# Two attention layers: constant rows and the first batch's rows in pieces, GpSimd's key rotation behind the statistics, bulk loads behind maxima transfers

## What is computed

```
x = x + xattn0(layernorm(x), ctx, ctx)      # rotary embedding on q and k, linear position bias per head
x = x + ffn0(layernorm(x))                  # every token goes to its best expert
x = x + xattn1(layernorm(x), ctx, ctx)      # learned q, k, v and output projections
x = x + ffn1(layernorm(x))                  # every expert takes its 128 best tokens of a batch
```

## Time and profile before

| | |
|---|---|
| median of 3 runs | 1086.34 us (1085.2 to 1089.04) |
| profiled execution | 1078.34 us, span 1076.5 us |
| layer 0's attention, in the span | 0.7 to 277 us |
| layer 1's attention, in the span | 515 to about 800 us |
| TensorE busy | 944.4 us, 88% |
| VectorE, ScalarE, GpSimd busy | 56%, 48%, 28% |
| mean granted TensorE clock | 0.953 |

### The profile page before, as it was taken

One profiled execution on the slowest core, in us unless ns is written; L12 is line 12 of the kernel. 1 busy time (PEld: TensorE's weight loads), 2 busy tenths in 40 slices (PEclk: granted clock), 3 DMA queues, 4 the chain that ended last, 5 costly groups with the idle time before them and its releaser, 6 DMA issues. The chain is left out here.

```text
span 1076.5 us, 17358 instructions
## 1 busy us (share of the span) xinstructions
PE 944.4 (88%) x6842; PEld 650.2 (60%) x6842; DVE 605.6 (56%) x1011; ACT 513.6 (48%) x777; POOL 300.5 (28%) x280
## 2 busy tenths in 40 slices
PE   0159999899798999999779999999979999999993
PEld 0023334343576999999653444444449999999993
DVE  7678979794432111110586766979314836655553
ACT  1027777678423322332326775767633035445550
POOL 5467843000001222221132122000000245554222
PEclk9999999899869999999997999999987999999997
DMA  9978372500439999996884061320006224555316
GB/s 159 234 206 200 94 195 58 96 4 4 153 134 373 325 338 345 339 345 220 186 202 91 33 119 62 73 51 4 4 2 236 79 59 133 141 169 146 98 21 175
DMA packets 52148, 158.96 MB, mean 148 GB/s; under 512 B 7792, under 2 KB 27888, under 8 KB 41392
## 3 DMA queue, kind: packets, MB, share of 16 engines
q1 hardware_dynamic: 35952, 121.96, 38.7%
q0 software_dynamic: 12912, 29.63, 11.3%
q10 hardware_dynamic: 3216, 6.43, 1.6%
HBM read 116.18 MB, written 40.76 MB: 146 GB/s over the span
## 5 line engine op out<-in xcount | busy, mean ns | idle before, releaser
L786 DVE TENSOR_REDUCE a_row_max<-ps_ring 128x2 f32<-128x1024 f32 x256 | 308.9, 1222 | 79.0 <-PE ps_ring L581 76.6
L719 ACT ACTIVATE a_probs<-ps_ring 128x1024 f32<-128x1024 f32 x256 | 260.7, 1022 | 102.1 <-PE ps_ring L596 100.2
L615 PE MATMUL ps_out<-a_probs,a_vaug 128*32 128x256 f32 x2048 | 166.7, 399 | 2.5 <-ACT a_out_sb L725 1.5
L581 PE MATMUL ps_ring<-a_ka,a_qa 52*128 52x512 f32 (+1 forms) x512 | 120.1, 473 | 54.4 <-DMA a_ka<-scratch_k_scr 44.2
L596 PE MATMUL ps_ring<-a_qa,a_ka 56*128 56x512 f32 (+1 forms) x512 | 131.7, 511 | 5.7 <-DMA a_qa<-a_max_t 3.7
L1056 ACT ACTIVATE e_hid<-ps_ring,e_wts 128x128 f32<-128x128 f32 x184 | 52.3, 368 | 120.2 <-PE ps_ring L1156 86.2
L596 PEld LDWEIGHTS ps_ring<-a_qa,a_ka 56*128 56x128 f32 (+1 forms) x512 | 49.1, 188 | 98.6 <-issue 67.3
L581 PEld LDWEIGHTS ps_ring<-a_ka,a_qa 52*128 52x128 f32 (+1 forms) x512 | 51.5, 199 | 86.9 <-issue 38.9
L1445 ACT ACTIVATE e_hr<-ps_ring 128x512 fp32r<-128x512 f32 x64 | 38.3, 598 | 118.9 <-PE ps_ring L1516 118.9
L1516 PE MATMUL ps_ring<-e_xt,e_wr 128*128 128x512 f32 x384 | 88.7, 390 | 0.4 <-DVE e_xt L1584 0.4
L615 PEld LDWEIGHTS ps_out<-a_probs,a_vaug 128*32 128x32 f32 x2048 | 41.1, 109 | 78.4 <-issue 72.2
(11 more groups left out here) (229 smaller groups left out, 1275.0 us busy)
## 6 DMA issues: line engine op xcount, KB each, us to landing
e_wts<-in_w SPq DMA_DIRECT2D x23, 1156.0 KB, 8.2
e_wts<-in_w SPq DMA_DIRECT2D x23, 1024.0 KB, 7.7
e_wf<-in_w SPq DMA_DIRECT2D x16, 1024.0 KB, 5.3
scratch_q_scr<-a_qst POOLq DMA_DIRECT2D x36, 256.0 KB, 3.2
a_qa<-scratch_q_scr SPq DMA_DIRECT2D x24, 384.0 KB, 10.2
a_ka<-scratch_k_scr SPq DMA_DIRECT2D x24, 384.0 KB, 12.2
scratch_k_scr<-a_kst POOLq DMA_DIRECT2D x9, 512.0 KB, 15.8
scratch_xl<-e_xn SPq DMA_DIRECT2D x8, 512.0 KB, 5.0
```

Of the source, the lines that this page charges most:

```text
L581: ins = pe.matmul(to[:, par], qa[rows, b % 2, g, p, qt * P:(qt + 1) * P], ka[rows, b % 2, g, p], start=True, stop=True)
L615: ins = pe.matmul(m.ps_out[VW * h:VW * (h + 1), cols], vaug[:, b % NV, kc, HG * g + h], probs[:, t % 3, h, cols], start=(kc == 0 and half ...
L719: nc.scalar.activation(probs[:, t % 3, 2 * half:2 * half + 2], unit("s", n), ACT.Exp, scale=HD ** -0.5).then_inc(exp_done, 1)
L786: dve.tensor_reduce(row_max[:, s % 3, qt, :, p], unit("m", n), AX.X, ALU.max).then_inc(mx_read, 1)
```

## The change

1. The constant rows come in three pieces: piece 0 is slot 0 of the batches, group 0; piece 1 is slot 0, groups 1 to 3; piece 2 is slot 1. In layer 0 each piece is six DMAs (16, 48 and 64 KB each), in layer 1 two. Piece 0 is issued without the wait for x; piece 1 by GpSimd behind query tile 0 (layer 0) or at once (layer 1); piece 2 in step -4, ahead of query tile 3. TensorE waits for each piece at its first use instead of for all.
2. Batch 0's rows are loaded in three parts: group 0, group 1, groups 2 and 3, twelve DMAs instead of eight.
3. In layer 0 GpSimd waits for `stats_done` 2 (the statistics of batches 1 to 3) before `keys(1)`.
4. A batch's loads are issued in steps 16b - 15 and 16b - 11 and behind the maxima transfers of their step (before: 16b - 14 and 16b - 12, ahead of them; for batch 1 steps 2 and 4). For batch 1 and for every second part they also wait for a maximum product, `mx_full`. Layer 1 loads batch 1's keys there too.
5. `normed` does its two tiles one step apart. Layer 0 gets 30 idle multiplications ahead of the loop.

```diff
         def groups(b, part):
-            cut = 1 if b == 0 else 2
-            return (0, cut) if part == 0 else (cut, NG)
+            if b == 0:
+                return ((0, 1), (1, 2), (2, NG))[part]
+            return ((0, 2), (2, NG))[part]
...
-                        if b >= 2:
+                        if b == 1:
+                            sp.wait_ge(mx_full, 8 + 1)
+                        elif b >= 2:
                             sp.wait_ge(st_full, 8 * NG * (b - 1))
-                    if layer == 1 and b >= 2:
+                    elif b:
+                        sp.wait_ge(mx_full, 8 * (NG * (b - 1) + groups(b, part)[0]) + 1)
+                    if layer == 1 and b:
                         load_keys(b, part)
...
-                for part in range(2):
+                for part in range(3):
                     load(0, part)
-                if layer == 1:
-                    for part in range(2):
-                        load_keys(1, part)
                 for t in steps:
...
-                        for part in range(2):
-                            if t == (2 if b == 1 else 16 * b - 14) + 2 * part:
-                                load(b, part)
                     for job in ended.get((t, 1), []):
                         if job[0] == "m":
                             load_max(job[1])
+                    for b in range(1, B):
+                        for part in range(2):
+                            if t == 16 * b - 15 + 4 * part:
+                                load(b, part)
...
-                if layer == 0:
-                    pool.wait_ge(x_in[0], 16)
...
+                def constant_rows(piece):
+
+                    f, g0, g1 = ((0, 0, 1), (0, 1, NG), (1, 0, NG))[piece]
+                    kinds = ((ka, QK_ROWS, "k_bias"), (qa, QK_ROWS, "q_bias"))[:2 if layer == 0 else 0] + ((ka, M_ROWS, "k_select"),)
+                    for dst, at, name in kinds:
+                        for par in range(2):
+                            src = dram[name] if name == "k_select" else dram[name][par]
+                            pool.dma_start(dst[par * HALF_P + at:par * HALF_P + at + 4, f, g0:g1].rearrange("r g p t -> r (g p t)"),
+                                           src[:, g0:g1].rearrange("r g p t -> r (g p t)")).then_inc(rows_in[piece % 2], 16)
+
+                constant_rows(0)
...
                     queries(0)
+                    constant_rows(1)
                     values(0)
+                    pool.wait_ge(stats_done, 2)
+                else:
+                    constant_rows(1)
                 for t in steps:
+                    if t == -4:
+                        constant_rows(2)
...
-                pe.wait_ge(rows_in, 16 * n_rows)
+                if layer == 0:
+                    keep_awake(30)
...
-                        if t == max(q_at[i] - 3, steps[0]):
-                            normed(i)
+                        for j in range(2):
+                            if t == max(q_at[i] - 4 + j, steps[0]):
+                                normed(i, j)
```

More of the change, by code:

```diff
@@ L207, in attention @@
             bo_ready = sem("bo_ready")
-        rows_in = sem("rows_in")
+        rows_in = [sem(f"rows_in{i}") for i in range(2)]
         vaug_set = sem("vaug_set")
@@ L235, in attention @@
         n_ctx = 2
-        n_rows = 6 if layer == 0 else 2
+        row_pieces = (0, 1, NG)
+        n_kinds = 3 if layer == 0 else 1
         k_scr = dram["k_scr"]
@@ L328, in rows_in_place, with landed @@
                                         scr[b].rearrange("r (d h) t -> (r d) (h t)", d=HD)[:, cols])
+                def landed(b, part):
+                    if b:
+                        return loaded[part]
+                    return (first_loaded, *loaded)[part]
                 def load_keys(b, part):
                     for par in range(2):
-                        rows_in_place(ka, k_scr, b, part, par).then_inc(k_loaded[b % 2][part], 16)
+                        rows_in_place(ka, k_scr, b, part, par).then_inc(landed(b, part), 16)
                 def load(b, part):
@@ L526, in keep_awake @@
                     for _ in range(n):
-                        pe.matmul(misc[:, 0:P], m.ident[:], m.ident[:], start=True, stop=True)
+                        pe.matmul((misc if layer else m.ps_out)[:, 0:P], m.ident[:], m.ident[:], start=True, stop=True)
                 def job_at(job, n):
@@ L570, in maxima_scores @@
                     b, g = s // NG, s % NG
-                    for part in range(2):
+                    for part in range(2 if b else 3):
                         if w == 0 and g == groups(b, part)[0]:
-                            if layer == 0:
-                                pe.wait_ge(loaded[part], 64 * (b + 1))
-                            else:
-                                pe.wait_ge(loaded[part], 32 * (b + 1))
-                                pe.wait_ge(k_loaded[b % 2][part], 32 * (b // 2 + 1))
+                            if s == 0:
+                                pe.wait_ge(first_loaded, 64)
+                            else:
+                                pe.wait_ge(loaded[part if b else part - 1], 64 * (b + 1))
+                            if s in row_pieces:
+                                piece = row_pieces.index(s)
+                                pe.wait_ge(rows_in[piece % 2], 32 * n_kinds * (piece // 2 + 1))
                     to = take_unit("m", n)
@@ L702, in _ @@
                     if job == (norm_kind, 0):
-                        normed(0)
-                        normed(1)
+                        for i in range(2):
+                            for j in range(2):
+                                normed(i, j)
                     act_job(job)
```

24 lines of the change are left out of this document (12 added, 12 removed).

## The result

| | before | after |
|---|---|---|
| median of the runs shown | 1087.69 us (1085.2 to 1089.82) | 1060.26 us (1053.83 to 1061.54) |
| profiled execution | 1078.34 | 1059.8 |
| its span | 1076.5 | 1058.0 |

The ratio is 0.9737 (95% interval 0.9691 to 0.9783). The kernel is faster, but the median lies 9.4 us under the forecast of 1069.7 and 3.7 us under the range. The profiled executions differ by 18.5 us, close to the 16.6 of my sum; the medians differ by 27.4.

A forecast was written before the change was run, and what follows sets the result against it. TensorE, mostly 90% busy, was taken to lose time waiting in the ramp, where constant rows hold the DMA queue, and for later transfers. Terms -8.2 - 5.6 + 1.9 + 1.0 - 3.2 - 2.0 - 0.5 = -16.6: median 1069.7 us, range 1064 to 1079.

The forecast's parts named there:

- Bulk behind the maxima: Step 8 scores wait for a maxima transfer behind bulk loads of batch 1; moving the loads gains 3.2 us (0 to 3.2).
- Constant rows in pieces: Start of layer 0: smaller pieces free SyncE's queue, so query stores land 8.2 us earlier (6.9 to 10.9).
- Three parts: Ramp: group 1's rows land right behind group 0's, the 8.4 us wait goes; 5.6 us gained, 3 if late.
- What is late next: Ramp: slot 0's maxima transfer, queued behind bulk loads, becomes the limit; 1.9 us given back (0 to 5).
- Piece 2, and the wait for statistics: GpSimd's chain and 384 KB of constant rows in layer 0: the wait costs nothing; 1.0 us lost for both (0 to 8).
- Rival (a): New wait in step 4 or 8 from late batch 1 rows or maxima; 6 to 8 us lost, about 1077; chance 0.20.
- (d): Slower: the last 384 KB of constant rows block the queue longer than their size suggests; 1088 to 1090; chance 0.07.
- `normed` in halves: ScalarE's 1.41 us piece split over two steps shortens TensorE's waits for an exponential; 2.0 us gained (0.5 to 3.5).
- Idle multiplications: TensorE at about 13 us: 0 on the path, ramp products stay at half speed; 2.2 us if they woke it.
- Layer 1: Layer 1's start: less queued ahead of the y rows, but VectorE sets the path; 0.5 us gained (-1 to 1.5).
- Rival (b): Start: input loads themselves, not the constant rows, cause the slow stretch; stores still land at 42, 1077 to 1079; chance 0.08.
- Rival (c): More is won: stores land at 31.3, no maxima wait, clock rises early; 1064 or less; chance 0.13.

The follow-up runs named there:

- the second profile: The kernel before, unchanged, measured and profiled once more: 1087.4 us, ratio 1.0032; its profiled execution took 1081.81 us.
- the context experiment: Kernel after with batch 2's context loaded behind slot 0's maxima transfer instead of ahead of it: 1062.47 us, beside 1062.31.
- the constant rows whole: Kernel after with all six constant-row transfers at the start and one TensorE wait for them, as before: 1068.73 us, ratio 0.9847.

## Why the prediction was wrong

**The step that failed is *Bulk behind the maxima*,** 3.2 us (0 to 3.2). It went wrong twice. I put the wait of 3.2 us into step 8 of batch 0; but the earlier trace rows has 0.43 there, and the wait of 3.2 stands in the timeline of before at batch 3:

```profile
205.12 0.80 PE L596 MATMUL ps_ring<-a_qa,a_ka 56*128 56x512 f32 x2 [3.23 <-DMA a_qa<-a_max_t]
...
207.28 0.79 PE L596 MATMUL ps_ring<-a_qa,a_ka 56*128 56x512 f32 x2
...
210.32 0.50 PE L596 MATMUL ps_ring<-a_qa,a_ka 56*128 56x512 f32 x2
```

And I took the wait for its price. Behind it the pairs stay at 0.80 us for 5 us, and the slot is 17.0 instead of 11.65: 5.3 us in this execution. Others lose more (18.6 and 15.3 in the second profile). Measured alone the part is 9.8 us, and 6.6 more than I gave it brings the sum from -16.6 to -23.2, against -23.0 measured. The split agrees: beside each other this part alone took 9.8 us off and the rest 13.0 (predicted 13.4). In the kernel after it is 16.4, because there the scores come 11.5 us earlier and batch 1's loads, in their old place, only 5.8 (74.96 instead of 80.78, behind GpSimd's chain), so that step 8 runs into them. It was a mechanism that I had named, with its place and its price wrong; the same wait of 3.2 also went into my time for step 8 (27.7 less 3.2 behind the scores), which came 27.1 us behind them, as before (27.7).

**The choice of the base failed with it.** I worked on a profile 8 us under the median and applied its sum to the median as if the 8 us were a constant. They were not: part of them were the losses that this change removes. In the second profile of before these are the 3.3 us more in the two slots; how much they are in the other executions no profile shows. The profile moved by 18.5 and the median of all executions by 23.0.

*Constant rows in pieces* (-8.2, range 6.9 to 10.9, less 2.6). Right in mechanism, too large: 5.75 us in the first loads of the two profiles (6.4 between the means of three profiles with the pieces and three without), 5.1 in the scores when only this part is undone, because both pieces held others up more than I took. Piece 0 kept the inputs back by 1.6 to 2.2 us (I took 0, at worst 2.6), and piece 1 the stores by about 5 (2.7: 34.0 against 31.3). And the part is worth nothing without the others. Why so few bytes hold others back, by the 4 partitions of each transfer, by GpSimd's queue or by something else, no run tested.

*Three parts* (-5.6). From first product to scores it was 25.3 and is 19.7 us: 5.6. The wait of 8.4 is gone.

*What is late next* (+1.9). Scores at 62.4 predicted, 62.84 measured, but this was luck: the maxima transfer was good for less than 1 us (the context experiment). What made the sum come out is that the pieces won less.

*Piece 2, and the wait for statistics* (+1.0, "the wait costs the path nothing"). The statistics were done at 32.75 instead of 31. The wait doesn't only cost nothing; it is worth 4 us of the ramp, which I had not seen. Batch 1's loads went out at 74.67 (predicted 73), step 8 began at 89.97 (predicted 86.9) and has no wait, and the slots before it (12.9 and 12.5) together are no longer than in before (12.35 and 12.9) by more than 0.2 us: of the 1.0 us little is seen. Rival (a) did not happen, nor did (d).

*`normed` in halves* (-2.0). About 1.5 us by slots, and the waits for the exponential 2.4 less; the medians can't tell.

*Idle multiplications* (0). Right: 1061.4 and 1061.6 us without them. I had offered 2.2 us if they woke the clock; to do that they must go on through the ramp, and then may bring 2 to 4 (1056 against 1058.1 and 1059.8), which is not shown, as the intervals overlap.

*Layer 1* (-0.5). Not shown. In the three profiles of the kernel after layer 1's attention takes 289.7, 285.0 and 285.3 us, in two of before 286.4 and 287.0.

Rival (b) is refuted by the constant rows whole: with everything else in place they alone bring the first loads from 36.5 back to 41.4. The Trainium skill ("DMA: Bandwidth & Descriptors", Anatomy of one DMA) puts a GpSimd DMA at about 2.0 us plus its bytes over 436 GB/s; that was the rival's other support, and the 5 us measured between the two kernels speak against it. Rival (c), 1064 or less, is what the median did, though not by its conditions: the stores landed at 36.5 and not at 31.3.

## What to carry to other kernels

A small transfer that an engine waits for belongs ahead of the bulk transfers of its queue, and its price here was not the wait alone but the half-speed stretch behind it too: read the distance between two equal marks of the loop (17.0 against 11.65), not the waits' sum. Before a sum goes onto a median, ask what the executions that are slower than the profiled one lose, since a change that removes a collision can gain more there. And work that is early on one engine can slow its neighbour: GpSimd 7.5 us earlier made VectorE's part 7.1 us later.

## What was not expected of the hardware

- 96 KB into 4 partitions at a time held back 4.8 MB of input by 2.2 us (about 1.6 over all profiles); 288 KB of them, issued from 21.25 us on, held back by about 5 us the landing of six stores of 256 KB issued from 25.24 on.
- Beside GpSimd's key rotation single VectorE instructions took 5.58 and 5.77 us that otherwise take 0.41 and 0.69, while GpSimd lost less than 1 us.
- TensorE's speed when the scores begin is not settled by the kernel: pairs of 0.80 us last 5.7 to 24.3 us from one execution to another, in one profile with TensorE busy throughout from 66 to 82 us at a granted clock of 0.50. The worst of it cost 5.7 us in two slots (15.7 and 15.4 instead of 12.9 and 12.5).
- Thirty idle multiplications at 13 us turn the granted clock of 30 to 70 us from 1.00 to 0.50 in the records, and change no duration and no median.
